# Cross attention with a state-space layer on one core: two DMA sums in turn, folded reciprocals, a projection two groups ahead and a reordered start

## The reference

```python
x = layernorm(builder, g1, beta1); base_n = layernorm(base, g1, beta1)
# _mha: 8 heads of 64; queries from x (4096 x 512), keys and values from base_n (3202 x 512)
scores = einsum('bhqd,bhkd->bhqk', q, k) / sqrt(64)
attn = softmax(scores, axis=-1)
out = einsum('bhqk,bhkd->bhqd', attn, v) @ W_o.T + b_o
x = builder + out
U = (layernorm(x, g2, beta2) @ W_in.T + b_in) @ Bmat
# scan over 4096 steps of 64 states: s = silu(s @ A.T) + u_t
x = x + states @ Cmat + (program_probs.mean(axis=1) @ W_prog.T + b_prog)
```

## Time and profile before

| | us |
|---|---|
| median of three runs (2385.86 to 2391.2) | 2390.56 |
| the profiled execution | 2387.81 |
| its span, first to last instruction | 2386.0 |
| prologue, up to the attention loop | about 330 |
| attention loop, 32 units | about 1845 |
| projection of 16 groups | about 135 |
| scan and output | about 75 |

### The profile page before, as it was taken

How to read it: one execution, slowest core, us unless ns; L and a number is a source line. 1 busy time by engine, 2 the same in 40 slices (tenths; PEclk the granted TensorE clock), 3 DMA queues, 4 the chain that set the end, 5 groups by cost and what they waited for, 6 DMA issues and landing times.

```text
span 2386.0 us, 36268 instructions
## 1 busy us (share of the span) xinstructions
PE 2311.1 (97%) x14506; PEld 1338.4 (56%) x14506; DVE 1666.3 (70%) x2129; ACT 1112.3 (47%) x1397; POOL 1634.4 (68%) x975
## 2 busy tenths in 40 slices
PE   7999989999999999999999999999999999999987
PEld 7998855555555555445455454545544555445754
DVE  5765557777777777777777777777777777664855
ACT  3654424444444444444444444444444444453454
POOL 1200038888888888888888888888888888886311
PEclk9999999999999999999999999999999999999987
DMA  6660225555555565555555655555555555666723
GB/s 232 199 195 10 80 71 114 116 121 119 115 121 119 131 137 130 130 121 119 120 123 135 138 139 134 120 124 115 115 115 118 122 119 120 150 142 156 234 80 141
DMA packets 130154, 306.55 MB, mean 128 GB/s; under 512 B 10241, under 2 KB 49793, under 8 KB 129346
## 3 DMA queue, kind: packets, MB, share of 16 engines
q0 software_dynamic: 46080, 167.79, 36.1%
q1 hardware_dynamic: 83906, 136.45, 16.3%
HBM read 87.54 MB, written 48.89 MB: 57 GB/s over the span
## 4 chain that ended last, share of the span: by engine, by line
PE 48%; POOL 20%; DMA 18%; issue 9%; DVE 4%; ACT 1%; POOLq 0%; SPq 0%; ACTq 0%; DVEq 0%
POOL accp L463 16%; DMA accd<-pt 14%; PE ps L1154 12%; PE ps L1051 5%; PE ps L1015 4%; PE ps L1137 3%; PE ps L1141 3%; PE ps L1139 3%; PE ps L1033 3%; PE ps L1023 3%; PE ps L1144 2%; DMA shb<-m_scratch 2%; PE ps L1211 2%; POOL accd L474 2%; PE ps L1267 1%
## 5 line engine op out<-in xcount | busy, mean ns | idle before, releaser
L463 POOL TENSOR_TENSOR accp<-accp,pt 128x1024 f32<-128x1024 f32 x512 | 1302.5, 2544 | 43.8 <-ACT pt L612 14.6
L785 DVE TENSOR_REDUCE mx_part<-ps 128x2 f32<-128x1024 f32 x768 | 939.8, 1224 | 451.0 <-PE ps L1051 450.9
L612 ACT ACTIVATE pt<-ps 128x1024 f32<-128x1024 f32 x800 | 780.3, 1023 | 935.0 <-PE ps L1144 916.5
L1154 PE MATMUL ps<-pt,v 128*64 128x512 f32 x3328 | 805.6, 605 | 0.0
L1154 PEld LDWEIGHTS ps<-pt,v 128*64 128x64 f32 x3328 | 201.8, 136 | 362.2 <-issue 315.6
L1051 PE MATMUL ps<-kk,qh 64*128 64x512 f32 x1536 | 345.3, 445 | 19.9 <-DVE mx_part L785 19.9
L1051 PEld LDWEIGHTS ps<-kk,qh 64*128 64x128 f32 x1536 | 143.7, 184 | 361.1 <-DVE mx_part L785 273.6
L1137 PE MATMUL ps<-qh,kk 64*128 64x512 f32 x1664 | 334.1, 397 | 0.8 <-ACT pt L612 0.8
L1141 PE MATMUL ps<-ql,kk 64*128 64x512 f32 x1664 | 328.8, 391 | 0.0
L1139 PE MATMUL ps<-qh,kk 64*128 64x512 f32 x1664 | 328.4, 390 | 0.0
L474 POOL DMA_DIRECT2D accd<-pt x256 | 229.1, 895 | 122.5 <-DMA accd<-pt 81.1
(11 more groups left out here) (146 smaller groups left out, 1834.7 us busy)
## 6 DMA issues: line engine op xcount, KB each, us to landing
accd<-pt POOLq DMA_DIRECT2D x288, 512.0 KB, 4.5
q_scratch<-kk SPq DMA_DIRECT2D x32, 512.0 KB, 4.1
shb<-m_scratch SPq DMA_DIRECT2D x32, 512.0 KB, 6.5
accd<-accp POOLq DMA_DIRECT2D x32, 512.0 KB, 5.1
o_scratch<-ost SPq DMA_DIRECT2D x32, 512.0 KB, 2.8
og<-o_scratch SPq DMA_DIRECT2D x32, 512.0 KB, 4.7
xs<-x SPq DMA_DIRECT2D x16, 512.0 KB, 6.5
qh<-q_scratch SPq DMA_DIRECT2D x32, 256.0 KB, 6.7
```

Source lines behind the costliest of these rows:

```text
L463: nc.gpsimd.tensor_tensor(acc[:, :], acc[:, :], pt[n % PT_SLOTS][:, :], ALU.add).then_inc(added_p, 1)
L612: nc.scalar.activation(pt[n % PT_SLOTS][:, :], src, ACT.Exp, scale=SCALE).then_inc(exped, 1)
L785: nc.vector.tensor_reduce(mx_part[:, m % QT, :, m // QT], src, AX_X, ALU.max).then_inc(max_taken, 1)
L1154: ins = mm(ps[HD * h:HD * (h + 1), 6, :], v[:, t, f:f + HD], pt[n % PT_SLOTS][:, h * QB:(h + 1) * QB], start=(t == 0), stop=(t == NT - 1))
```

## The change

- **Shift.** `V_STEPS` grows from seven to nine steps (3 to 11 in place of 2, 3, 7 to 11), so nine tiles of a unit in place of seven get their shift from VectorE. Where the shift is a matmul, it now comes ahead of the scores, save for tile 0. `shb` has one buffer in place of two.
- **Sums.** Seven tiles go by DMA into `acca`, five by DMA into `accb`, in turn; 14 stay on GpSimd, which adds `accb` to `accp` at the end of the unit (`add_b`), then sends `accp` to `acca`. `PT_SLOTS` falls from 7 to 6.
- **Reciprocals.** ACT copies the spread sum out of bank 7 (`take_den`), SP folds one row of each head to 64 x 8 (`fold_den`), VectorE inverts 128 x 8, SP stores that and spreads it over the partitions (`spread_rden`), and GpSimd scales `oraw` behind tile 18.
- **Projection.** `project(d + 2)` runs before `turn2(d)`. `fold_den` and `spread_rden` of the last unit stand in groups 4 and 6 of SP's queue, the constants of the last stage are loaded in group 7, and the steps behind them move one to three groups later.
- **Prologue.** Two x groups are loaded before the query weights; the first two groups are normalized together; ACT scales the weights before it normalizes; `bias(0)` is split around the first `turn`; for groups 0 and 1 the next `turn` stands between two halves of `project_q`.

The core of the diff:

```diff
-D_TILES = [2, 5, 8, 11, 13, 16, 19, 21, 24]
-P_TILES = [t for t in range(NT) if t not in D_TILES]
-PT_SLOTS = 7
-V_STEPS = [2, 3, 7, 8, 9, 10, 11]
+A_TILES = [1, 5, 9, 13, 17, 21, 24]
+B_TILES = [3, 7, 11, 15, 19]
+P_TILES = [t for t in range(NT) if t not in A_TILES + B_TILES]
+P_SUMS = len(P_TILES) + 1
+PT_SLOTS = 6
+V_STEPS = [3, 4, 5, 6, 7, 8, 9, 10, 11]
...
+            def fold_den(u):
+                sp.wait_ge(den_taken, u + 1)
+                for h in (0, 1):
+                    sp.dma_start(den8[HD * h:HD * (h + 1), :],
+                                 den_sb[HD * h:HD * h + 1, :].rearrange("o (p j) -> o p j", j=8)).then_inc(den8_loaded, 16)
+
+            def spread_rden(u):
+                sp.wait_ge(rden_ready, u + 1)
+                sp.dma_start(r_scratch[u % 2].rearrange("h (p j) -> (h p) j", j=8), rden8[:, :]).then_inc(rden_stored, 16)
+                sp.wait_ge(rden_stored, 16 * (u + 1))
+                wait(sp, o_scaled, u)
+                for h in (0, 1):
+                    sp.dma_start(rdenb[HD * h:HD * (h + 1), :], r_scratch[u % 2, h:h + 1].to_broadcast([HD, QB]))\
+                        .then_inc(rdenb_loaded, 16)
...
-            for n in (1, 2, 3):
+            for n in (2, 3):
                 load_xs(n)
...
                 if u > 0:
+                    fold_den(u - 1)
+                    spread_rden(u - 1)
                     store_o(u - 1)
...
-                if d == 5:
-                    sp.wait_ge(sum_spread, UNITS)
+                if d == 4:
+                    fold_den(UNITS - 1)
+                if d == 6:
+                    spread_rden(UNITS - 1)
+                if d == 7:
                     sp.dma_start(cb_sb[:, :, :], ctxb).then_inc(mod_loaded, 16)
...
+            def add_b(u):
+                acc = accp[u % 2]
+                pool.wait_ge(added_b, 16 * len(B_TILES) * (u + 1))
+                pool.wait_ge(added_p, P_SUMS * (u + 1) - 1)
+                nc.gpsimd.tensor_tensor(acc[:, :], acc[:, :], accb[:, :], ALU.add).then_inc(added_p, 1)
...
+            def scale_o(u):
+                pool.wait_ge(rdenb_loaded, 32 * (u + 1))
+                pool.wait_ge(o_taken, u + 1)
+                nc.gpsimd.tensor_tensor(oraw[:, :], oraw[:, :], rdenb[:, :], ALU.mult).then_inc(o_scaled, 1)
...
+            def take_den(u):
+                act.wait_ge(sum_spread, u + 1)
+                wait(act, den8_loaded, 32 * u)
+                nc.scalar.activation(den_sb[0:HD + 1, :], ps[0:HD + 1, 7, :], ACT.Copy).then_inc(den_taken, 1)
...
-            def invert(u, i):
-                dve.wait_ge(sum_spread, u + 1)
-                c = slice(i * P, (i + 1) * P)
-                nc.vector.reciprocal(ps[:, 7, c], ps[:, 7, c]).then_inc(rden_ready, 1)
+            def invert(u):
+                dve.wait_ge(den8_loaded, 32 * (u + 1))
+                wait(dve, rden_stored, 16 * u)
+                nc.vector.reciprocal(rden8[:, :], den8[:, :]).then_inc(rden_ready, 1)
...
+                    if u > 0 and j == 6:
+                        invert(u - 1)
...
-                if n + 1 < NG:
+                if 1 < n < NG - 1:
                     turn(n + 1)
...
+                    if n < 2:
+                        project_q(n, range(2))
+                        turn(n + 1)
+                        project_q(n, range(2, FC))
...
+                    if j in V_STEPS:
+                        open_tile(u, 2 * j)
+                        shift_scores(u, 2 * j, True)
+                        open_tile(u, 2 * j + 1)
+                        scores(u, 2 * j + 1, True, True)
+                    else:
+                        score_tile(u, 2 * j)
...
-            project(0, 0)
-            project(0, 1)
+            for d in (0, 1):
+                project(d, 0)
+                project(d, 1)
             for d in range(X_G):
-                if d + 1 < X_G:
-                    project(d + 1, 0)
+                if d + 2 < X_G:
+                    project(d + 2, 0)
```

More of the change, by code:

```diff
@@ L873, in low_wo @@
                     .then_inc(wo_lo, 1)
-            def between(u, j):
-                if j in V_STEPS:
-                    add_shift(u, 2 * j + 1)
-                if u > 0 and j in (4, 5):
-                    invert(u - 1, 2 * (j - 4))
-                if u > 0 and j == 6:
-                    scale_o(u - 1)
-            def behind(u, j):
-                if u > 0 and j in (4, 5):
-                    invert(u - 1, 2 * (j - 4) + 1)
             for u in range(UNITS):
@@ L924, in _ @@
                 project(d)
-                if d in (3, 4):
-                    for i in (2 * (d - 3), 2 * (d - 3) + 1):
-                        invert(UNITS - 1, i)
                 if d == 5:
-                    scale_o(UNITS - 1)
-                if d == 8:
+                    invert(UNITS - 1)
+                if d == 9:
+                    dve.wait_ge(o_scaled, UNITS)
+                if d == 10:
                     dve.wait_ge(mod_loaded, 16 * 6)
@@ L1000, in turn, with bias @@
                         ins.then_inc(turned, 1)
-            def bias(w):
+            def bias(w, columns):
                 pe.wait_ge(w_loaded[w], 16)
-                for m in range(FC):
+                for m in columns:
                     for k in range(FC):
@@ L1140, in scores, with score_tile @@
                 for h, r in enumerate(rows):
-                    ins = mm(ps[:, b + h, :], kk[r, p, 0, key], ql[u % 2][r, :], start=False, stop=t in V_TILES)
-                if t not in V_TILES:
-                    for h, r in enumerate(rows):
-                        ins = mm(ps[:, b + h, :], ones_row[r, :], sh[u % 2][r, :], start=False, stop=True)
-                ins.then_inc(scored, 1)
+                    ins = mm(ps[:, b + h, :], kk[r, p, 0, key], ql[u % 2][r, :], start=False, stop=last)
+                if last:
+                    ins.then_inc(scored, 1)
+            def score_tile(u, t):
+                open_tile(u, t)
+                if t == 0:
+                    scores(u, t, True, False)
+                    shift_scores(u, t, False)
+                else:
+                    shift_scores(u, t, True)
+                    scores(u, t, False, True)
             def pv(u, t):
@@ L1163, in spread_sum @@
                 for h in (0, 1):
-                    ins = mm(ps[HD * h:HD * (h + 1), 7, :], ones[:, :], accd[u % 2][:, h * QB:(h + 1) * QB], start=True, stop=True)
+                    ins = mm(ps[HD * h:HD * (h + 1), 7, :], ones[:, :], acca[u % 2][:, h * QB:(h + 1) * QB], start=True, stop=True)
                 ins.then_inc(sum_spread, 1)
```

198 lines of the change are left out of this document (120 added, 78 removed).

## The result

The kernel after the change takes 2375.32 us (median of 4 runs, 2373.33 to 2377.75), the kernel before, on the same chip, 2390.68 (4 runs, 2385.86 to 2391.2). The ratio is 0.9941, 95% interval 0.9923 to 0.9958: faster by 0.6%, some 15 us. I had said 2364, in a range of 2348 to 2386. So the side and the range held, and 11 of the 26 us that I had promised are missing. The profiled execution has a span of 2375.9 us against 2386.0.

The account below looks back on a forecast made before the run. The prediction saw two loop limits within 2%, TensorE's work and GpSimd's round with its DMAs. Terms -16 - 15 + 0 - 7 + 12 = -26 took 2387.8 to 2361.8; with 2.8 for the median, 2364 us, range 2348 to 2386.

Parts of the forecast that it names:

- Shift matmuls: Attention loop, TensorE: two more steps with VectorE shifts save 14.4 us, plus 1.5 in the last unit; together -16 us.
- Sums: Attention loop, GpSimd: a second DMA chain removes most waits for accumulating transfers; -15 us, bounds -22.5 and 0.
- The 4 us kept for unit 30 and the 3 to 4 for the tight start of a unit: Loop losses expected to remain: unit 30, where weights and x also load, and tight pt slots at unit starts.
- Rival 2: Loop keeps its waits through the lost slot and higher DMA load; only matmuls and prologue gain: 2379 us, chance 0.14.
- rival 3: Loop: accumulating transfers from GpSimd's queue run one after the other, 58.5 us a unit; slower, 2418 us, chance 0.07.
- Folded reciprocals: Attention loop: the folded denominators arrive before VectorE comes for them, so no effect; 0, bounds 0 and +1 us a unit.
- rival 4: Loop: the fold comes late, VectorE stands at invert and TensorE behind it; 2395 us, chance 0.06.
- Prologue: Kernel start: first projection at 18.1 instead of 25.21, gain handed on; -7 us, bounds -5 and -8.
- Projection: After the loop: longer lead saves 5.7 us, but SP queue waits, context sum and clock cost more; +12, bounds -5 and +18.
- The two waits that I priced: Projection: og queued behind fold_den before group 5, +7.2 us, and behind spread_rden before group 7, +4.3 us.
- The clock: Projection: each of the two long TensorE waits costs about 2 us more at the lower clock, +4 us.
- Rival 1: Projection: SP is not what TensorE waits for, og comes in time and the lead pays; -3 there, 2349 us, chance 0.13.

Follow-up runs that it names:

- seven_steps: The changed kernel with V_STEPS back to seven steps (2, 3, 7 to 11), all else as changed: 2388.2 us, 0.9986 on the kernel before.
- before_nine: The kernel before with only nine VectorE shift steps and the shift ahead of the scores in each bank: 2424.47 us, 1.0149 on the kernel before.
- one_sum_seven: The changed kernel with one DMA sum of nine tiles, no add_b, and V_STEPS back to seven: 2472.65 us, 1.0346 on the kernel before.
- high_o_early: The changed kernel with one line moved, ACT's high_o(31) one group earlier, at 7 instead of 8: 2365.97 us, 0.9907 on the kernel before.
- tail_queue: The changed kernel with SP's tail reordered (fold_den, spread_rden, store_o, constants later; scale_o, high_o, mean product moved to fit): 2349.9 us, 0.9831 on the kernel before.
- og_later: The changed kernel with only the last unit's four og loads moved behind spread_rden(30): 2371.3 us, 0.9916 on the kernel before.
- tail_og: The changed kernel with both SP's tail reordered and the last unit's four og loads behind spread_rden(30): 2345.75 us, 0.9817 on the kernel before.
- old_prologue: The changed kernel with the prologue of before: 2381.43 us, 0.9967 on the kernel before.
- best2: As tail_og, with x1 of groups 0 and 1 added before either normalization and the context sum in two halves: 2343.88 us, 0.9807 on the kernel before.
- one_sum: The changed kernel with one DMA sum of nine tiles, 16 GpSimd additions and no add_b: 2473.31 us, 1.0339 on the kernel before.

## Why the prediction came out as it did

**Shift matmuls, -16.** The 14.4 us of the loop measured 14.7 (seven_steps). The 1.5 for the last unit didn't show, since og loads made that unit longer. But the sentence "it is all on the path while TensorE is the limit, and I find nothing that hides it" hid a condition: alone on the kernel before, the shifts cost 36 us (before_nine, 2424.47 against 2388.75), and with one sum they are worth nothing (one_sum_seven).

**Sums, -15.** The mechanism is shown: the waits of L480 and L474 went, down to 21.7 and 10.8 us, which no longer hold TensorE, and the loop from before to seven_steps is 20.0 us shorter. The 4 us kept for unit 30 and the 3 to 4 for the tight start of a unit were not needed. So the two loop terms gave 34.7 us, where I had 29 to 31. Rival 2 (the waits stay) is out, and rival 3 too: 13 transfers a unit of 4.6 to 4.9 each would make over 59 us in turn, and the unit is 56.5.

**Folded reciprocals, 0.** As a price this is right: VectorE doesn't wait for den8 anywhere, rival 4 is out. As a value it is wrong. By the order of the rows (the folded reciprocals were not tried alone) it takes 3.8 us of reciprocals and the scaling off VectorE in steps 4 to 6, which is what makes room for the shift additions there, and it puts scale_o on GpSimd, which only the second sum makes room for. I saw "VectorE gets lighter", but on average, not in the two steps where it counts.

**Prologue, -7.** 17.75 where I had 18.1: the weights came 1.2 us later, not 1.6. Of the 7.5 at the first projection 5.7 reached the loop in the two traces, and 6.1 is the difference of the medians.

**Projection, +12, measured +26.7.** This is the term that failed: the mechanism was right, the size was not, since three of the five waits were missing from it. The two waits that I priced came as priced: 7.18 before group 5 for my 7.2, 4.53 before group 7 for my 4.3. Missing were:
- The wait before group 11, 9.8 us and 1.5 at the lower clock. Of all that SP waits for in its tail I walked fold_den and spread_rden, but not store_o(31), whose chain runs over GpSimd to ACT's high_o, which the change itself had put two groups later (high_o_early: 9.4 us).
- The wait before group 8: 1.8 us and 1.6 at the lower clock. SP issues six constants ahead of that og, from 2199.39 to 2203.04; that they are the cause is read from the rows, no run moved them alone.
- The og of group 2: 2.5. It can be loaded only once the first projection has left its slot, and with a landing of 6 us that is later than TensorE wants it.
- The clock: I took 2 us for each of two waits; the four waits cost 2.6, 1.6, 1.6 and 1.5, so 7.4 for my 4.
Against that the 2 us for the context sum did not show, since the wait for group 11 lay over it; with the queue in order it is there (2.69 in tail_queue, before group 12, at x1 of group 11). Sum by the two traces: 25.9 of waits for og; all other waits of TensorE there 8.2 where they were 14.1, so -5.9 for my -5.7; and TensorE busy for 132.2 where it was 125.7, so +6.6, the slower matmuls. That makes 26.6 against 26.7 measured. The rule of the Trainium skill that I named (TensorE: Matmul & The Clock Gate, HAM oscillation) bears on this: a wait for DMA is paid again behind it. The traces agree for four of the five waits, not for the one of 2.54: the clock in the stretch was 0.90, against 0.97 in tail_queue without the four.

**The last unit** was priced as part of the loop at -3 and came at +2.5: 2 MB of og loads at its start, which also stood there before, now meet two chains of accumulating transfers (og_later: 4.0 us). In its first 26 us a tile's transfer took 5.8 us before the change and 7.8 into acca after it, medians of three.

Rival 1, "SP is not what TensorE waits for", was set at 2349, and tail_queue, in which that is nearly so (2.5 us for og are left), took 2349.9. The match is partly luck: its projection took 139.1 us, 0.6 less than before and not 3, and its loop gave 34.9 for my 29 to 31.

**The total** held its range although the projection cost 15 us more than I had put, because the loop gave 4 to 6 more; by the medians 11 of the 26 us are missing.

## What to carry to other kernels

When an engine is made to run one group further ahead, walk every queue whose entries are placed by group number, not only those with a new entry: ACT's high_o, put at group 8 where it had stood at 6, stopped, over GpSimd and SP, a load that has nothing to do with it. Ahead of a load that a busy engine needs, put no DMA that waits for another engine; two groups later cost nothing here.
Parts of a change that load different engines aren't a sum. Here the shifts alone lost 1.5%, and the kernel with folded reciprocals, a slot less and no second sum (one_sum_seven) took 1.8 us more a unit than the one before, while the three together took the loop to TensorE's bound. Price each by what is then longest, and for an engine close to full do it for the step with the most work, not for the mean.

## What the hardware showed that I had not expected

- Waits of like length are followed by the lower clock or not: in the projection 2.54 us (changed kernel) and 2.69 (tail_queue) left the tiles behind at full speed (5.74 for two, 2.96 for one), while 2.54 (high_o_early), 2.71 and 3.02 (tail_og) did not (7.15 for two, 4.43 for one, 7.35 for two). In the other traces 2.56 (old_prologue) and 2.59 (best2) were followed by it, 2.47 (seven_steps) and 2.56 (og_later) were not. All waits for og of 4.2 and more were. Among the shorter ones, 1.81 us in the changed kernel was (4.62 for one tile, ten us behind another such wait), 1.85 in high_o_early was not. What decides in between, no run here shows.
- More DMA load as such didn't slow the loop: the engines' mean share rose from 0.56 to 0.71, and the median landing of a tile from 4.5 to 4.9 us (acca) and 4.6 (accb). The landings of 8 us in the changed kernel's last unit stand beside a burst of 2 MB; before the change one of 7.27 is in the chain in the middle of the loop.
- GpSimd's additions take 2470 ns in the changed kernel, where they mostly wait for their tile, and 2563 in one_sum, where they stand back to back; the instruction is the same. No run here tells why.
